# A graph-attention kernel: the chain that makes a batch's logits moved into the ten steps before that batch's weighing, its links one or two sums apart

## What is computed

```
def _gat_layer(h, W, al, ar, src, dst, residual):
    feat = (h @ W).reshape(N, H, D)            # H = 4 heads of D = 64
    el = jnp.sum(feat * al[None], axis=-1)
    er = jnp.sum(feat * ar[None], axis=-1)
    e = jax.nn.leaky_relu(el[src] + er[dst], NEG_SLOPE)
    m = jax.ops.segment_max(e, dst, num_segments=N)
    ex = jnp.exp(e - m[dst])
    den = jax.ops.segment_sum(ex, dst, num_segments=N)
    a = ex / jnp.maximum(den[dst], jnp.asarray(1e-09, ex.dtype))
    out = jax.ops.segment_sum(a[:, :, None] * feat[src], dst, num_segments=N)
    ...
```

## Time and profile before

| | |
|---|---|
| time, median of 3 runs | 8175.72 us (8173.67 to 8177.49) |
| the profiled execution | 8176.97 us, its span in the trace 8175.2 us |
| the three attention layers, first exponential to last | 3117.5 to 6930.1 us |
| batches | 156 |
| busy share of the span | PE 64%, POOL 59%, DVE 52%, ACT 37% |
| mean granted TensorE clock | 0.73 of full speed |

### The profile page before, as it was taken

The page is one execution under the profiler, slowest core; times in us unless marked ns, Lnnn a source line. Parts: engine busy times, 40 slices in busy tenths (PEclk is TensorE's granted clock), DMA queues, the critical chain, the costliest instruction groups (busy, mean ns, idle before and its releaser), DMA issues. The chain is left out here.

```text
span 8175.2 us, 88909 instructions
## 1 busy us (share of the span) xinstructions
PE 5192.9 (64%) x16844; PEld 3062.5 (37%) x16844; DVE 4260.4 (52%) x11715; ACT 2988.4 (37%) x11762; POOL 4805.2 (59%) x5023
## 2 busy tenths in 40 slices
PE   3976666655555664677674767765666666456565
PEld 1434444433333332444442444433344444233333
DVE  3124444444444464666665666665566667444444
ACT  0310000000000034777775777775677777000000
POOL 0036666656666626666664666664666665666665
PEclk9977777767767776766766676776677777666666
DMA  3443333323333324444443444444444443333333
GB/s 110 148 132 102 101 103 101 101 84 93 92 93 92 92 68 149 119 120 118 120 122 86 116 121 117 122 120 123 113 119 121 118 120 94 94 98 98 99 98 85
DMA packets 413383, 883.38 MB, mean 108 GB/s; under 512 B 95067, under 2 KB 231813, under 8 KB 412870
## 3 DMA queue, kind: packets, MB, share of 16 engines
q0 software_dynamic: 240176, 662.04, 29.6%
q1 hardware_dynamic: 128048, 172.59, 6.3%
q10 hardware_dynamic: 44646, 43.24, 1.7%
HBM read 775.32 MB, written 102.18 MB: 107 GB/s over the span
## 5 line engine op out<-in xcount | busy, mean ns | idle before, releaser
L439 POOL DMA_INDIRECT rows_a<-table,rows_src x4160 | 4005.8, 963 | 2375.3 <-issue 933.6
L543 PE MATMUL ps<-rows_a,hot_a 128*128 128x256 f32 (+1 forms) x4992 | 1918.2, 518 | 1119.6 <-issue 734.0
L1820 ACT ACTIVATE rows_a<-rows_a,ex_a 128x64 f32<-128x64 f32 x9984 | 2475.5, 338 | 338.9 <-issue 335.2
L1880 PE MATMUL ps<-rows_a,hot_a 128*128 128x260 f32 x4992 | 2135.4, 553 | 324.5 <-DVE agg L1738 212.2
L506 DVE TENSOR_TENSOR agg<-agg,ps 128x256 f32 (+1 forms) x2496 | 1047.6, 420 | 1981.1 <-remote 1033.7
L543 PEld LDWEIGHTS ps<-rows_a,hot_a 128*128 128x128 f32 x4992 | 1098.4, 247 | 1867.2 <-issue 1115.6
L1738 DVE TENSOR_TENSOR agg<-agg,ps 128x260 f32 x2496 | 1043.9, 418 | 1077.1 <-PE ps L1880 602.6
L1880 PEld LDWEIGHTS ps<-rows_a,hot_a 128*128 128x128 f32 x4992 | 1120.2, 259 | 685.5 <-issue 463.1
L439 POOL DMA_INDIRECT rows_a<-table,row x832 | 789.3, 949 | 413.4 <-issue 179.5
L1964 ACT ACTIVATE root_a<-mv_a,eps 128x1 f32<-128x1 f32 x49 | 14.4, 295 | 1194.8 <-issue 639.3
L490 DVE TENSOR_TENSOR hot_a<-ps,dloc 128x1024 f32<-128x1024 f32 x312 | 379.2, 1217 | 0.0
(11 more groups left out here) (282 smaller groups left out, 3791.9 us busy)
## 6 DMA issues: line engine op xcount, KB each, us to landing
dstt_a<-dloc_dram SPq DMA_DIRECT2D x156, 512.0 KB
rows_a<-table,rows_src POOLq DMA_INDIRECT x4160
table<-ob SPq DMA_DIRECT2D x50, 1024.0 KB, 4.4
rows_a<-table,row POOLq DMA_INDIRECT x832
table<-ob_n SPq DMA_DIRECT2D x98, 130.0 KB
x_dram<-cur ACTq DMA_DIRECT2D x1, 6400.0 KB
cur<-x_dram ACTq DMA_DIRECT2D x1, 6400.0 KB
table<-obg SPq DMA_DIRECT2D x49, 130.0 KB, 2.1
```

The costliest lines, as they stand in the source:

```text
L439: nc.gpsimd.indirect_dma_start(out=rows[:, n % ring, 0:width], out_offset=None, in_=table, in_offset=bass.IndirectOffsetOnAxis(ap=index[:, ...
L543: nc.tensor.matmul(ps[n % banks][:, 0:width], hot[:, m % nbuf, j, :], rows[:, n % RING, :], start=True, stop=True).then_inc(step_done, 1)
L1820: ins = nc.scalar.mul(a, a, ex[:, k % GV, s, h:h + 1])
L1880: nc.tensor.matmul(ps[j % banks][:, 0:W4], hot[:, j, :], rows[:, k % GV * UG + j, :], start=True, stop=True).then_inc(step_done, 1)
```

## The change

It moves calls in the two hand-written loops and adds or removes none of a batch's instructions. On DVE `logit_parts(n)` now stands behind A3 of batch k = n - 1 (before: behind A10 of batch n - 2), `within_rows` behind A5 (A0), `across_rows` behind A7 (A2), `tops` behind A9 (A5), `edge_sums` and `logits` behind A12 (A9), `growth` behind A13 (A11), `edge_hots(n + 1)` behind A14 (A12). On PE `turn` stands behind S4 (S0), `turn_ends` behind S6 (S2), `turn_carries` behind S8 (S5), `turn_tops` behind S10 (S8), and the first groups of `er_of_edges` behind S0, S2, S5 and S7 (S0, S3, S6 and S7).

```
@@ DVE
                 logits(0)
                 one_hots(0, 0)
                 growth(0)
-                logit_parts(1)
                 acc = accs(0, 0)
                 for k in range(KG):
                     n = k + 1 if k + 1 < KG else None
                     rescale(k, acc[0])
                     accumulate(k, 0, acc[0])
-                    if n:
-                        within_rows(n)
                     accumulate(k, 1, acc[1])
                     one_hots(k, 1)
                     accumulate(k, 2, acc[2])
-                    if n:
-                        across_rows(n)
                     accumulate(k, 3, acc[3])
                     acc = accs(k, 1)
+                    if n:
+                        logit_parts(n)
                     accumulate(k, 4, acc[0])
                     accumulate(k, 5, acc[1])
                     if n:
-                        tops(n)
+                        within_rows(n)
                     accumulate(k, 6, acc[2])
                     accumulate(k, 7, acc[3])
                     if n:
+                        across_rows(n)
                         one_hots(n, 0)
                     acc = accs(k, 2)
                     accumulate(k, 8, acc[0])
                     accumulate(k, 9, acc[1])
                     if n:
+                        tops(n)
+                    accumulate(k, 10, acc[2])
+                    accumulate(k, 11, acc[3])
+                    acc = accs(k, 3)
+                    accumulate(k, 12, acc[0])
+                    if n:
                         edge_sums(n)
                         logits(n)
-                    accumulate(k, 10, acc[2])
-                    if n and n + 1 < KG:
-                        logit_parts(n + 1)
-                    accumulate(k, 11, acc[3])
+                    accumulate(k, 13, acc[1])
                     if n:
                         growth(n)
-                    acc = accs(k, 3)
-                    accumulate(k, 12, acc[0])
+                    accumulate(k, 14, acc[2])
+                    if n:
+                        first = accs(n, 0)
                     if n and n + 1 < KG:
                         edge_hots(n + 1)
-                    for j in range(13, 16):
-                        accumulate(k, j, acc[j - 12])
-                        if j == 14 and n:
-                            first = accs(n, 0)
+                    accumulate(k, 15, acc[3])
                     acc = first
@@ PE
                     sums(k, 0, 1)
                     if n:
-                        turn(n)
                         er_of_edges(n, 0, er_rows(n, 0))
                     sums(k, 1, 3)
                     if n:
-                        turn_ends(n)
-                    sums(k, 3, 4)
+                        er_of_edges(n, 1, er_rows(n, 1))
+                    sums(k, 3, 5)
                     if n:
-                        er_of_edges(n, 1, er_rows(n, 1))
-                    sums(k, 4, 6)
+                        turn(n)
+                    sums(k, 5, 6)
                     if n:
-                        turn_carries(n)
+                        er_of_edges(n, 2, er_rows(n, 2))
                     sums(k, 6, 7)
                     if n:
-                        er_of_edges(n, 2, er_rows(n, 2))
+                        turn_ends(n)
                     sums(k, 7, 8)
                     if n:
                         er_of_edges(n, 3, er_rows(n, 3))
                     sums(k, 8, 9)
                     if n:
+                        turn_carries(n)
+                    sums(k, 9, 11)
+                    if n:
                         turn_tops(n)
-                    sums(k, 9, 15)
+                    sums(k, 11, 15)
                     if n:
                         factor(n)
                     sums(k, 15, 16)
```

49 lines of the change are left out of this document (25 added, 24 removed).

## The result

The changed kernel took 8361.54 us (median of 4 executions, 8360.1 to 8371.23), the kernel before on the same chip 8176.6 us (8173.67 to 8178.37). The ratio is 1.0229, with a 95% interval of 1.0211 to 1.0247: **slower by 185 us**. The forecast was slower by 380.

What follows compares the result with a forecast made beforehand. The pair PE and DVE was taken to set the pace, 23.5 us a batch. Terms 7.3 + 9.0 + 9.8 made 26.1 us, 382 us more over 147 periods: 8555 us, range 8020 to 8900.

Steps and rivals of the forecast that it cites:

- the shape: DVE idles ahead of A5, A7, A9 and A11, and A1 follows A0 without a hole.
- the idle time ahead of all additions: Sign on DVE: its idle time ahead of additions grows by about 400 us in all.
- term (b): The four links between PE and DVE, from `el` to the next exponential, without the products' return times: 9.0 us a period.
- L: Time from a product's start on PE to the start of its addition, where DVE waits for it: 2.44 us taken.
- term (c): Return time of the products behind the four links, S5, S7, S9 and S11: four times 2.44, 9.8 us a period.
- wrong about the price: Sign against the forecast: additions behind a link start within 1.3 us of their product.
- closes, 1.91 us here: DVE's hole ahead of A1 goes, 1.91 us, since `turn` no longer stands behind S0 waiting for the rescale.
- term (a): From the exponential to `el` written, A10 to A12 and A0 to A3 on DVE: 7.3 us a period.
- prompt products: Rival: products behind links return promptly; period 22.3 us, time 8001 us, or 21.3 and 7853 with 1.24 at all four; chance 0.21.
- all layers alike: The three attention layers each go from 23.5 to 26.1 us a period, over 147 periods together.
- The rival's 3.80 us at all four links: Late products: PE's idling keeps its clock at 1.2 GHz; period 31.5 us, time 9353 us; chance 0.15 for over 8800.

Runs made afterwards that it cites:

- after_turns_later: The changed kernel with each of PE's four turns of the chain two products later, on a fast chip: 7211.1 us, 1.0115 of the kernel before.
- before_no_cast: The kernel before with SP's 512 KB broadcast cut to 16 bytes per partition from the third batch on, on a fast chip: 7133.5 us, ratio 1.0001.
- All four edits: The changed kernel with PE's turns one product later, three register loads behind work, layer three's inversion later and output copy earlier: 7151.42 us, 1.0003 on a fast chip.
- after_again: The changed kernel as it is, run again on a fast chip: 7401.91 us, 1.0379 of the kernel before.

## Why the prediction was right and wrong

**Right: direction, and in part the shape.** It said slower, and that DVE would wait ahead of A5, A7, A9 and A11 and no longer ahead of A1. The idle times over the three layers are 0.65, 0.69, 0.30 and 1.17 us a batch there, 2.8 together (1.1 before), and 0.26 at A1 where it was 2.1. POOL and ACT wait more for what comes out of the loop, as foreseen. But the idle time ahead of all additions should have grown by about 400 us and grew by 40 (968 to 1008 over the 147 periods): what came at the links and ahead of A3 is about what went at A1 and elsewhere. That near links cost time is shown on the fast chip, by `after_turns_later`: only the number of products that PE has issued when it stops for a link was changed, and 2.6 of the 3.8% came back. The exposed loads are shown there too (1.5%). On a slow chip the two were only taken back together.

**Right to the tenth: term (b), the links without L.** From `el` written (3606.18) to the next exponential (3619.87) the batch above takes 13.69 us. The mean of layers one and two is 13.7. The prediction's 9.0 with four L as measured (1.11 to 1.27, together 4.8) is 13.8.

**Wrong: term (c), L four times.** I took the mean of 3.80, 2.28 and 1.24, 2.44, because "these products come back in the same setting, alone behind a link". They don't. L behind a link is 1.1 to 1.3 us at S5, S7, S9 and S11 on average, which the prediction had named as the sign of being wrong about the price. The three rows had two things in them: L, which is the smallest of them, and a wait that comes on top. S1 itself shows it. On the fast chip, in `before_no_cast`, it comes back in 1.24 to 1.25 us in all 147 periods; on the chip of the result it needs 2.9 us on average, over 2 us in 98 of 147 and under 1.35 in 36. The 3.80 has the hole in it, and the 2.28 lies between. The term should have been 4 x 1.24 = 5.0 and not 9.8; it measured 4.8. The estimate by TensorE: Matmul & The Clock Gate, section Single matmul latency, in the Trainium skill, 1.05 us, was nearer than my mean: the trace has 0.1 to 0.3 us more where PE was waiting for a link at the lower clock. A spread of 1 to 3 in three rows should have been read as two mechanisms, and the lowest as the price of one.

**Wrong: the hole "closes, 1.91 us here".** It does not belong to the link at S1. The very batch that the prediction read has a longer wait at another place, ahead of A9, with ACT held up beside DVE, by two transposes that PE's records end at 3731.25:

```profile
3735.07 0.38 ACT L1289 ACTIVATE xt_n<-ps 128x256 f32<-128x256 f32 x1 [2.43 <-remote]
3735.11 0.43 DVE L1738 TENSOR_TENSOR agg<-agg,ps 128x260 f32 x1 [2.48 <-PE ps L1880]
```

Such waits come in all kernels on the slow chips, at A1 above all in the kernel before. In the changed kernel they come ahead of A3 (2.5 us a batch in layers one and two) and lie inside term (a): 2.8 us in the batch above, between 3601.49 and 3604.29. Term (a) also counted a register load ahead of `el` at 0.52, as it was ahead of A15; it is 1.2 us there, since nothing covers it. Together (a) was 10.7 us, measured from exponential to `el`, and not 7.3.

The two parts as measured are 10.7 + 13.7 = 24.4 us. The two errors, - 5.0 in (c) and + 3.4 in (a), left + 0.9 us a period in layers one and two and not + 2.6, a third of it; layer three lost 1.9, which is why the whole came out at half the size. That it came so near is luck: the two errors have nothing to do with each other. On a fast chip, where no hole is, the sum 7.3 + 9.0 + 5.0 = 21.3 stands beside a measured 21.2, by a smaller luck: (a) is 7.8 there, with the load ahead of `el`, and the rest 13.4. The rival "prompt products" had this figure, and its price (about 1.2 at all four) is what was measured. It came out slower than before and not faster, because the hole stayed where there is one, and because the kernel before runs at 20.2 where there is none.

**Wrong: all layers alike.** Layer three lost twice as much as each of the others on the slow chip (25.4 against 24.4), and 24.1 against 21.2 on the fast one. The prediction called the finished blocks' work unchanged. Its place is, but it stands at fixed steps of DVE and PE and waits for ACT, and ACT's exponential now comes later against those steps. All four edits are worth 3.4 us a batch there between the two fast chips (24.1 and 20.7).

**The clock.** The section The HAM clock gate of that page in the Trainium skill says that PE's clock falls when PE idles, and I had taken that as a rival. The direction shows: in layer two on fast chips the granted clock is 0.77 in `before_no_cast`, 0.73 with the four links, 0.83 with the turns two products later. There is a price, and it is small. In `after_again` S5 comes back in 0.68 us when the clock is at its full level of 2.4 GHz (67 of 98 batches of layers one and two) and in 1.13 us at the lower level (23 of them). One of the first sort, S5, A5 and the stretch between (granted clock 1.00):

```profile
2832.10 0.64 PE L1879 MATMUL ps<-rows_a,hot_a 128*128 128x260 f32 x2
...
2832.78 0.42 DVE L1738 TENSOR_TENSOR agg<-agg,ps 128x260 f32 x1
```

```profile
2832.10:2832.80 0.70, 0.64 (x3) 0.23 (x2) 0.56 (x3) 0.70 (x5) 0.44 (x1) 1.00 0.54 161
```

S7, S9 and S11 stand at the lower level in most batches of either chip, so the 1.24 us of the rows had this price in it already. The rival's 3.80 us at all four links did not come.

**Not settled:** what the hole is. It was shown that on a slow chip cutting the broadcast or every second gather doesn't remove it, that it strikes whatever PE has finished, and that two chips don't have it. The transfers that bring instructions (queue q14 of the profile's page) don't go with it: in the changed kernel a packet of that queue starts in the 6 us ahead of the end of 27% of DVE's waits of over 1.5 us for products, and in the 6 us ahead of 30% of moments taken at random. Whether it has to do with PE's clock was not tried.

## What to carry to other kernels

A round trip between two engines costs its latency once for each link, unless the first engine has the other's next inputs under way before it stops for the link. The distance that counts is the one on the queue of the engine that stops: here, on a fast chip, the turn belongs two products behind the place that reads naturally. Put a load of registers behind an instruction, never ahead of the one that the chain waits for. And when one price varies by three between equal places, look for a second mechanism that lands there by chance, before a mean of it is multiplied by four.

## What the runs showed of the hardware

- The same program took 7131, 7150, 8177 and 8243 us on four chips, and a change can be worth 2.3% on one kind and 3.8% on the other. In the attention layers the difference (3.3 us a batch, some 480 us in all) goes with stalls of about 3 us in which nothing that PE has finished reaches DVE, ACT or POOL. The profile books them as "remote" or as a wait for PE long done. On the fast chips the waits from 3500 to 4300 us have no "remote" row in any of the ten runs.
- The other half of the difference lies in the parts that the change doesn't touch, and there the same kind of wait shows: DVE's additions of `aggregate` (L506) stand idle for some 510 us more on a slow chip, half of their idle time is booked as "remote", and on a fast chip none is. First `before`, then `before_no_cast`:

```profile
L506 DVE TENSOR_TENSOR agg<-agg,ps 128x256 f32 (+1 forms) x2496 | 1047.6, 420 | 1981.1 <-remote 1033.7
```

```profile
L506 DVE TENSOR_TENSOR agg<-agg,ps 128x256 f32 (+1 forms) x2496 | 1048.1, 420 | 1467.5 <-PE ps L543 1450.1
```

- A product of two matmuls, 128x260, that nobody else delays reaches DVE's addition 0.68 us behind its start at the full clock and 1.13 us at the lower one (S5 in `after_again`).
- A load of four block numbers into DVE's registers keeps what stands behind it on the queue back by 0.5 us (`hott`) to 1.2 us (`el`), and holds up less where it runs under an instruction: with three loads moved, `hott` doesn't wait and `el` waits 0.5 us.
- An indirect gather of 16 rows holds POOL nearly as long as one of 128: the mean over both sorts, half and half, is 926 ns, against 969 for 128 rows alone.
